# Second attention: reciprocal denominators spread by two transfers through DRAM instead of a diagonal, a product and a copy

## What is computed

```
q = (text_hidden @ Wq).reshape(B, T_text, N_HEADS, HEAD_DIM).transpose(0, 2, 1, 3)
...
scores = jnp.einsum('bhtd,bhsd->bhts', q, k) / scale
scores = jnp.where(mask, scores, -jnp.inf)
attn = jax.nn.softmax(scores, axis=-1)
...
out = jnp.einsum('bhts,bhsd->bhtd', attn, v)
out = out.transpose(0, 2, 1, 3).reshape(B, T_text, N_HEADS * HEAD_DIM)
return out @ Wo
```

## Time and profile before

| what | value |
|---|---|
| device time, median of 3 runs | 1621.13 us (1619.86 to 1626.16) |
| the profiled execution's own time | 1623.28 us |
| its span, first to last instruction | 1622.0 us |
| PE busy | 1412.5 us, 87% |
| DVE busy | 1233.2 us, 76% |
| ACT busy | 1104.4 us, 68% |
| POOL busy | 805.2 us, 50% |

### The profile page before, as it was taken

The page is one execution under the profiler, slowest core; times in us unless marked ns, Lnnn a source line. Parts: engine busy times, 40 slices in busy tenths (PEclk is TensorE's granted clock), DMA queues, the critical chain, the costliest instruction groups (busy, mean ns, idle before and its releaser), DMA issues.

```text
span 1622.0 us, 25718 instructions
## 1 busy us (share of the span) xinstructions
PE 1412.5 (87%) x8502; PEld 695.3 (43%) x8588; DVE 1233.2 (76%) x2247; ACT 1104.4 (68%) x2028; POOL 805.2 (50%) x664
## 2 busy tenths in 40 slices
PE   5788788888888888788899988899988999899999
PEld 3243243343333343244455544445543446454455
DVE  6667667767786256688999586979689997899857
ACT  4657656756755755487788586778587876787844
POOL 4014013014040022178778468687497875587843
PEclk9798998999988999899999999999999999999999
DMA  4001200300340100100000000000010000000000
GB/s 159 1 1 38 46 2 1 62 2 1 63 183 1 53 1 6 36 27 6 1 1 1 21 1 26 1 2 21 1 27 27 1 27 1 27 1 1 1 1 27
DMA packets 20491, 36.72 MB, mean 23 GB/s; under 512 B 4898, under 2 KB 15238, under 8 KB 19334
## 3 DMA queue, kind: packets, MB, share of 16 engines
q1 hardware_dynamic: 20358, 35.07, 7.4%
HBM read 26.53 MB, written 1.15 MB: 17 GB/s over the span
## 4 chain that ended last, share of the span: by engine, by line
PE 32%; DVE 9%; issue 7%; POOL 7%; ACT 4%; DVEq 0%; ACTq 0%; POOLq 0%
PE BK L722 32%; DVE arena L1719 4%; POOL arena L2118 4%; DVE arena L1700 2%; ACT arena L1982 1%; ACT arena L1975 1%; POOL arena L2124 1%; POOL arena L2115 1%; ACT arena L1993 1%; ACT L1975 0%; DVE arena L2307 0%; POOL arena L2103 0%; POOL arena L2092 0%; DVE arena L1071 0%; DVE arena L2313 0%
## 5 line engine op out<-in xcount | busy, mean ns | idle before, releaser
L722 PE MATMUL BK<-arena 128*128 128x512 bf16 (+11 forms) x8172 | 1366.5, 367 | 174.1 <-DVE arena L1537 39.3
L722 PEld LDWEIGHTS BK<-arena 128*128 128x128 bf16 (+6 forms) x8258 | 659.0, 111 | 852.0 <-issue 213.9
L2118 POOL TENSOR_TENSOR arena<-arena 128x512 f32<-128x512 f32 (+1 forms) x352 | 506.2, 1438 | 155.1 <-ACT arena L1975 132.9
L1719 DVE TENSOR_TENSOR arena<-arena 128x512 bf16<-128x512 f32 (+1 forms) x416 | 498.4, 1206 | 31.6 <-ACT arena L1982 30.4
L1975 ACT ACTIVATE arena<-BK,arena 128x512 f32<-128x512 f32 (+1 forms) x416 | 286.8, 689 | 128.7 <-PE BK L722 112.8
L1873 ACT ACTIVATE arena<-BK 128x512 f32<-128x512 f32 (+1 forms) x416 | 227.3, 604 | 92.7 <-PE BK L722 87.1
L1537 DVE TENSOR_REDUCE arena<-BK 128x1 f32<-128x512 f32 x384 | 244.5, 684 | 59.7 <-PE BK L722 58.6
L1982 ACT CAST arena<-arena 128x512 bf16<-128x512 f32 (+1 forms) x416 | 254.1, 611 | 0.0
L1700 DVE CUSTOM_DVE_ANT_0 arena<-BK,arena 128x512 bf16<-128x512 f32 (+1 forms) x256 | 145.1, 567 | 40.1 <-PE BK L722 39.8
L1993 ACT ACTIVATE arena<-BK 128x512 bf16<-128x512 f32 (+1 forms) x256 | 130.9, 512 | 58.1 <-PE BK L722 56.8
L2029 POOL TENSOR_TENSOR arena<-arena 128x256 f32<-128x256 f32 (+6 forms) x45 | 30.2, 671 | 186.4 <-ACT arena L1810 184.1
(11 more groups left out here) (179 smaller groups left out, 876.3 us busy)
## 6 DMA issues: line engine op xcount, KB each, us to landing
arena<-arena SPq DMA_DIRECT2D x144, 50.0 KB, 2.2
arena<-in_ctxT SPq DMA_DIRECT2D x8, 800.5 KB, 4.5
arena<-in_ctxk SPq DMA_DIRECT2D x4, 768.0 KB
arena<-in_wo SPq DMA_DIRECT2D x1, 2048.0 KB, 7.4
arena<-in_wqT SPq DMA_DIRECT2D x1, 2048.0 KB, 7.5
arena<-in_x SPq DMA_DIRECT2D x4, 256.0 KB, 9.8
arena<-in_rsel SPq DMA_DIRECT2D x1, 1024.0 KB, 9.4
arena<-in_rw1T SPq DMA_DIRECT2D x1, 1024.0 KB, 5.2
```

What stands on the lines that cost most here:

```text
L722: return T.matmul(out_, lhsT, rhs, start=start, stop=stop, skip_group_check=True)
L1719: V.tensor_tensor(Pl[k][0:m, :], P1[k][0:m, :], Ph[k][0:m, :], ALU.subtract).then_inc(p_low, 1)
L2118: G.tensor_tensor(acc[0:m, g % 2, :], acc[0:m, g % 2, :], P1[k][0:m, :], ALU.add).then_inc(summed1, 1)
```

## The change

For each group the diagonal on POOL, the product with ones on PE and the copy on ACT are gone. In their place SP writes the four reciprocals of each partition, 16 bytes, to a row `rowf` of 512 numbers in DRAM, waits for that to land, and then reads the row into all 128 partitions of `rc`. The row lies in the order (p u), so DVE's product reads `rc` with a step of four elements.

```
         def finish(g):
             last = g == NG - 1
             piece("o1a", g, bank=7)
-            yield
-            yield
+            piece("o1b", g)
             if last:
                 piece("xh", 0)
-                self.fill(4, "o1p", B - 1, 0)
-                piece("o1h", 0)
-            piece("o1b", g, bank=7)
-            yield
-            if last:
-                self.fill(5, "o1p", B - 1, 1)
-                piece("o1h", 1)
+                for t in range(2):
+                    self.fill(4 + t, "o1p", B - 1, t)
+                    piece("o1h", t)
+            yield
+            yield
+            yield
+            yield
             piece("o1c", g)
...
-                elif kind == "o1b":
-                    g, = arg
-                    pe.wait_ge(diag_done, g + 1)
-                    mm(BK[7][:, :], ones[:, :], dg[:, :, :].rearrange("p u n -> p (u n)")).then_inc(full[7], 1)
...
                 elif kind == "o1a":
                     dve.wait_ge(full[7], n + 1)
+                    dve.wait_ge(recip_out, 16 * arg[0])
...
-                    dve.wait_ge(*emptied("o1b", g))
+                    dve.wait_ge(recip_row, 16 * (g + 1))
...
-                    V.tensor_tensor(oN[:, h:h + 2, :].rearrange("p h n -> p (h n)"), BK[j][:, :], rc[:, :],
-                                    ALU.mult).then_inc(pv_taken, 1)
+                    V.tensor_tensor(oN[:, h:h + 2, :].rearrange("p h (t n) -> p (h t) n", t=2), BK[j][:, :].rearrange("p (u n) -> p u n", u=4),
+                                    rc[:, :].rearrange("p (n u) -> p u n", u=4), ALU.mult).then_inc(pv_taken, 1)
...
-                elif kind == "o1b":
-                    g, = arg
-                    act.wait_ge(full[7], n + 1)
-                    act.wait_ge(pv_taken, g)
-                    A.copy(rc[:, :], BK[7][:, :]).then_inc(free[7], 1)
...
-                elif kind == "o1a":
-                    g, = arg
-                    pool.wait_ge(dn_recip, g + 1)
-                    if g:
-                        pool.wait_ge(*filled("o1b", g - 1))
-                    G.tensor_tensor(dg[:, :, :], idn[:, :].unsqueeze(1).to_broadcast([128, 4, 128]),
-                                    dn[:, 4:8].unsqueeze(2).to_broadcast([128, 4, 128]), ALU.mult).then_inc(diag_done, 1)
...
+                elif kind == "o1b":
+                    g, = arg
+                    sp.wait_ge(dn_recip, g + 1)
+                    sp.wait_ge(recip_row, 16 * g)
+                    SP.dma_start(rowf.rearrange("(p u) -> p u", u=4), dn[:, 4:8]).then_inc(recip_out, 16)
+                    sp.wait_ge(recip_out, 16 * (g + 1))
+                    sp.wait_ge(pv_taken, g)
+                    SP.dma_start(rc[:, :], rowf.partition_broadcast(128)).then_inc(recip_row, 16)
```

More of the change, by code:

```diff
@@ L548, in finish @@
             piece("o1a", g, bank=7)
+            piece("o1b", g)
+            if last:
+                piece("xh", 0)
+                for t in range(2):
+                    self.fill(4 + t, "o1p", B - 1, t)
+                    piece("o1h", t)
             yield
             yield
-            if last:
-                piece("xh", 0)
-                self.fill(4, "o1p", B - 1, 0)
-                piece("o1h", 0)
-            piece("o1b", g, bank=7)
             yield
-            if last:
-                self.fill(5, "o1p", B - 1, 1)
-                piece("o1h", 1)
+            yield
             piece("o1c", g)
@@ L861, in program @@
         acc = sb("acc", [128, 2, 512], F32, L1)
-        dg = sb("dg", [128, 4, 128], F32, SM)
         rc = sb("rc", [128, 512], F32, L1)
@@ L890, in program @@
         rowd = [nc.dram_tensor(f"rowd{i}", (16, 128), BF16, kind="Internal").ap() for i in range(2)]
+        rowf = nc.dram_tensor("rowf", (512,), F32, kind="Internal").ap()
         xv = a["x"].rearrange("(t p) d -> p t d", p=128)
@@ L1106, in program @@
         ac_done = sem("ac_done")
-        mcb_done, q_high, max1_done, p_high, p_low, summed1, pv_done, diag_done, ck_high, ck_low, tern_done = (
+        mcb_done, q_high, max1_done, p_high, p_low, summed1, pv_done, recip_out, recip_row, ck_high, ck_low, tern_done = (
             sem(n) for n in ("mcb_done", "q_high", "max1_done", "p_high", "p_low", "summed1", "pv_done",
-                             "diag_done", "ck_high", "ck_low", "tern_done"))
+                             "recip_out", "recip_row", "ck_high", "ck_low", "tern_done"))
         l1_set, t_lt, t_half, dn_recip, pv_taken = (sem(n) for n in ("l1_set", "t_lt", "t_half", "dn_recip", "pv_taken"))
```

## The result

The changed kernel takes 1637.88 us (median of 7 runs, 1631.24 to 1646.78), the kernel before 1623.29 in the same session (7 runs, 1619.86 to 1627.43). The ratio is 1.0078, 95% interval 1.0053 to 1.0104: slower by 13 us, where 30 us less were forecast. The profiled execution has a span of 1630.9 us, one of the shorter ones of this kernel.

A forecast was written before the change was run, and what follows sets the result against it. PE was taken to bound the kernel, DVE close behind. Product with ones 21.5, diagonal waits 10, clock 3.4, less 2 for queued loads and 2.7 for `ln2`, gave 30.2 us: from 1621.13 to 1591 us, range 1576 to 1609.

The forecast's parts named there:

- PE's 0.86 us a group: PE's product with ones: removing it frees 0.86 us, all gained in undisturbed groups; 21.5 us remain over the kernel.
- The gain of 34.9 us in all: Gains before costs: PE's product with ones 21.5, waits for the diagonal 10, half-clock stretches 3.4 us.
- The transfers: 5.1 us forecast: SP's write and read of the denominators: 1.6 + 3.3 + 0.2 = 5.1 us, hidden under 6.8 us before `o1c`.
- `o1c` itself ... I book nothing: DVE's stepped read of `rc`: between nothing and a doubling of 0.68 us, DVE still under PE's 22.29; booked nothing.
- Rival B: DVE becomes the bound within a group, `o1c` growing by the 16-byte line rule: 16 us gained, 1605; chance 0.20.
- 6.9 us a group, which I put down to work beside POOL: DVE's full-size `r1`, 1.245 us against `o1c`'s 0.68: with less POOL work DVE needs about 0.5 us less; nothing booked.
- SP ... Nothing: SP's queue while the write lands: delayed loads are needed most of a group later, so no cost.
- -2.7 for `ln2`: Layer norm: PE waits for `ln2`, 0.9 us, right ahead of `ln3`, three times; cost 2.7 us.
- the clock, 3.4 us gained: Half-clock stretches behind three long PE waits cost 1.7 us each; two should go, gaining 3.4 us.

The follow-up runs named there:

- e1_gone: Kernel before without the diagonal, the product with ones and ACT's copy, nothing in their place (rc set to 1.0 once): 1592.8 us, ratio 0.9779.
- e13_free: Changed kernel with rc read in one run (denominators in wrong order), mask row load one piece earlier, ln2 ahead of the fifth tile: 1589.89 us, ratio 0.9785.
- e2_run: Changed kernel with rc read in one run instead of a step of four, so denominators are in the wrong order: 1608.73 us, ratio 0.9878.
- e14_turn: Changed kernel, stepped read kept, plus one POOL wait: its sum of the eleventh tile starts only after o1c has ended: 1623.49 us, ratio 0.9984.
- e16_seven: Changed kernel with rc read in one run (denominators in wrong order) and o1c cut into 7 pieces: ratio 0.9984.
- e9_norm: Changed kernel with o1a's weights read in steps of four, rc in one run, and ln2 ahead of the next group's fifth tile: 1633.55 us, ratio 1.005.

## Why the prediction was wrong

The range was 1576 to 1609, the time is 1637.88. The ratios line up as a ladder (a difference of two carries some 5 us of uncertainty):

| step | from | to | cost |
|---|---|---|---|
| removal alone | 1 | 0.9779 (e1_gone) | -36 us |
| the two transfers | 0.9779 | 0.9785 (e13_free) | 1 us |
| mask row and `ln2` late | 0.9785 | 0.9878 (e2_run) | 15 us |
| `o1c` 0.4 us longer, race won | 0.9878 | 0.9984 (e14_turn, e16_seven) | 17 us |
| race lost | 0.9984 | 1.0078 (changed) | 15 us |

**Right.** PE's 0.86 us a group: the period of an undisturbed group fell by 0.83 in e1_gone. The gain of 34.9 us in all, measured 36. The transfers: 5.1 us forecast, 5.4 measured (the write 1.46 where 1.6 was taken, the read 3.9 where 3.3 was taken and 3.8 was the bound), hidden as said: `o1c` comes at 7.2, forecast 6.8. The Trainium skill (DMA: Bandwidth & Descriptors, Anatomy of one DMA) gives its fixed cost of about 2.0 us for transfers issued by GpSimd, a condition that the prediction left out. These are SP's, and this write takes 1.46 us to the next issue.

**Wrong, the main step: "`o1c` itself ... I book nothing".** The bound was good, a doubling of 0.68; 1.09 came. Put at nothing, it costs 32 us, the last two steps of the ladder. The reasoning behind it failed: DVE's 21.7 us was compared with PE's 22.29 as if a group's mean load decided. Within the group `r1` stands right behind `o1c`, PE's `v1` right behind `r1`, and the place had 0.37 us to POOL's next sum, less than the 0.41 added. Rival B came nearest: it named the rule of the 16-byte lines, the "`o1c` of 1.0 us or more" and a PE idle for `r1` in undisturbed groups as its signs, and all three came; the period is 23.6, where it had 22.8. Its price, 1605, was too low by the race: it took DVE's time as a fluid, and a lost turn costs what is left of POOL's instruction, 1.1 us in an undisturbed group. It had no term for the mask row, `ln2`'s half clock and the new long waits either.

**Wrong for the same reason: what was said of `r1`.** "6.9 us a group, which I put down to work beside POOL" was the right row, read as a slowdown that falls with POOL's load. It is a queue of two. DVE's busy time did fall when POOL had an instruction less (21.49 to 21.11 in e1_gone's group, 0.4; 0.5 was said), but what matters is which of the two comes first at each `r1`.

**Wrong: "SP ... Nothing", and -2.7 for `ln2`.** The sentence on SP's queue looked at what comes late in a group and missed the mask row, which DVE needs within 5 us. For `ln2` the waits were right in number, three, and in kind, but 8.5 us in place of 4.6 + 2.7 = 7.3, and with half-clock work behind two of them; 8 us in all by e9_norm.

**Wrong in sign: the clock, 3.4 us gained.** From the first group's reciprocals to the last's the granted clock, summed over its records, is below full for 47.8 us in 11 stretches, before for 13.7 in 4; in e1_gone 6.8 in 2, so the term was right for the removal. Ahead of each of the 11 stretches PE had stood for 2.5 to 5.2 us; four other waits, of 2.8 to 3.4 us, had none behind them. The long waits did not go, as the term had it; of 2.5 us or more there are 15, before 3.

**Left open.** What the won race costs, 17 us, is by the intervals not to be told from the 13 us of DVE time (32 x 0.41), but why DVE's time should count in full is open: in an undisturbed group the period grows by 0.2 us only. e14_turn has 3.4 us more at half clock than e2_run (23.9 against 20.5), which accounts for 1.7; the rest may be other races in the groups with background work. In 16 to 18 of the 31 full groups `r1` behind `o1c` lasts over 1.2 us in e2_run, in e14_turn and in e16_seven already. No run separates them, nor the 10 of the 15 us of the lost race that lie outside the undisturbed groups.

## What to carry over

Where two engines exclude each other instruction by instruction, a mean load tells nothing of what a few tenths of a microsecond cost. Look in the timeline for who starts next on the other engine and by how much: here 0.37 us of room, and behind it a cliff of 1.1 us in each undisturbed group, five of 32, with twice as much in longer waits and half-clock work elsewhere. When data come out of a transfer in another order, price the step at each place where it could stand (the engine's read, its write, a weight load, the transfer's pieces) before choosing: over one plain run they cost here 32, 7, 36 and 214 us. And list what stands behind a new wait on SP by who needs it soonest, not by how much of it there is.

## What had not been expected of the hardware

An `r1` that starts 0.01 us behind POOL's sum by the records can still come first; at 0.03 to 0.04 us behind, both orders occur, and at 0.08 it came second; the loser is the one whose record grows (POOL's sum 1.82 us, or `r1` 1.73). A stepped float32 read of 16 bytes costs VectorE 0.41 us in 512 columns, a stepped bank read and SBUF write of 512 bytes 0.38, of which 0.07 overlap with the next instruction (`r1` starts 0.15 us ahead of `o1c`'s end, elsewhere 0.08). Cutting one instruction of 0.68 us into seven costs 0.39. The write of 2 KB from 128 partitions lets SP issue again after 1.46 us in pieces of 16 bytes and after 8.4 in pieces of 4.
